# Decoder layer on one core: x turned by VectorE, three weights split in the mixing stage, the residual stored with its bias

## The chip, the cores and the metric

The kernel runs on one core of one Trainium2 chip. A core has TensorE (PE, matrix products), VectorE (DVE), ScalarE (ACT), GpSimd (POOL) and SyncE (SP), which here issues all the DMA transfers. Each engine works through its own queue in order, and semaphores are the only coupling between them. The metric is the device time of one execution in microseconds: 967.11 us before (median of 3 runs, 964.91 to 968.43). Lower is better.

## The reference

x is (8, 512, 512) in float32: 8 batches of 512 tokens. ctx is (8, 77, 512). The layer has three parts, each followed by a residual addition and a layer norm.

```python
# 1 mixing: 8 heads of 64
q, k, v = split(x @ w_qkv)
kv = cumsum(fft(k) * fft(v), over tokens)
x = layernorm(x + real(ifft(kv * conj(fft(q)))) @ w_out)
# 2 cross attention: 16 heads of 32 over 77 keys, masked softmax
q, k, v = x @ W_q + b_q, ctx @ W_k + b_k, ctx @ W_v + b_v
x = layernorm(x + softmax(mask(q k^T / sqrt(32))) v @ W_o + b_o)
# 3 feed forward with an int4-rounded weight and a low-rank term
w = clip(round(kernel / scale), -8, 7) * scale      # scale = max|kernel| / 7
x = layernorm(x + x @ w + bias + (x @ a) @ b)
```

## The kernel before, in words

Every float32 product is made as three products of a high part and a low part ("split": the high part is a copy to a format that TensorE reads in one pass, the low part is what is left): `split_matmuls` (L58) issues hi*hi, lo*hi and hi*lo for each of four 128-row chunks, so one product of a 128x512 tile is 12 matmuls. The program has three stages. Each ends in a barrier of all engines.

**prepare** (L69) works on weights. It folds the Fourier transform into w_qkv (PE turns 128x128 blocks of w_qkv, multiplies with the transform; the result is split into `w_spec`) and into w_out (`w_back`, `fold_back`), turns ctx and, in the last four entries of `SIDE` (L138), the x of batch 0; projects and stores the keys in 8 pieces (`project_keys`, `bias_keys`, `split_keys`, n = 0 to 7); rounds the FFN weight and adds the low-rank term (`merge`, L484). It also splits W_o, W_v and the finished FFN weight (ACT `split_o`, `split_v`, `split_ffn`; low parts on POOL and DVE) and stores the six parts to DRAM (`w_later`), in SP's queue between the keys' stores; the last two stores are L227 and L228. `partition_all_reduce` (L418) on POOL finds the largest |kernel|, and DVE waits for it before L498. The stage ends when SP has seen all its stores land.

**mix_tokens** (L570) takes one batch per step, i = 0 to 7; steps 2 to 5 are a loop of two. In a step PE makes twelve projections of 12 matmuls (2 pairs x {V, K, Q} x 2 halves) and four back projections (`project_back`) of the batch before. The first half of PE's order (L714) is V V K K Q, back 0, Q, back 1, V, back 2, V, back 3, and the second half K K Q Q. Between the first K, K, Q and back 0 stand four `turn` calls (L672), each four 128x128 transposes, which bring the x of the next batch into the bank `xT_ps`; ACT copies the high part (L780), DVE makes the low part (L899). DVE multiplies (`times_k`, `times_q`), runs the prefix sum (`scan`, L921 and L923), adds the residual x to a back projection (`add_residual`, L948), measures and normalises (L963); POOL adds the two halves of the values (L847), makes their low part (L853) and raises the variance to -1/2 (`root`, L838). `project_back(i, t)` waits for `r_added` of tile t-1, that is for DVE's `add_residual` of the tile before, since there is one bank `out_ps`. `add_residual(i, 0)` waits for the transfer into the single tile `x_res`.

The places that set SP's order are `load_x` (into two x tiles; the load of batch i+3 waits until batch i+1 is turned), `load_residual(i)` (waits until batch i-1 has used `x_res`) and `store` (four tiles of x1, waiting for DVE's normalised tiles).

**attend** (L1097) makes, per step, the scores of one batch and the output projections, FFN and norms of the batch before. Four PSUM banks are handed round in the order `BANK_ORDER` (L1030): `O0, P00, O1, P01, O2, T0, ...` are an output projection, a turned piece of the probabilities, and so on; the fifth use needs the first to be emptied. At the start of each step POOL adds b_o to the four tiles of the loaded residual (`bias_residual`, L1714) and only then scales the probabilities (`normalize_probs`, L1706), which PE turns in `turn_probs` (L1322). `add_o` (L1908) on DVE adds the biased residual. The first residual load (L1257) waits for all values to be stored, because both use one tile, and is queued behind 4 MB of weights.

## Time and profile before

| | us |
|---|---|
| median of 3 runs | 967.11 (964.91 to 968.43) |
| the profiled execution | 967.57 |
| its span, first to last instruction | 965.8 |

Busy shares of the span: PE 94%, PE's weight loads 78%, DVE 69%, ACT 39%, POOL 35%; the mean granted TensorE clock is 0.977 of full speed. A share is an average over three stages with different limits, so the rows below are given by stage. In a row of the timeline the first number is the start in us, the second the duration; brackets hold the idle time before it and what ended it. The stages begin at 0, 75.8 and about 464 us.

### The profile page before, as it was taken

What the parts mean: (1) busy time and instruction counts of PE and PEld (TensorE: products, weight loads), DVE (VectorE), ACT (ScalarE), POOL (GpSimd) and SP (SyncE); (2) the same over time, 40 slices, a digit from 0 to 9 for tenths busy, and PEclk for the clock granted to TensorE, in tenths of its full rate; (3) what the DMA queues carried; (4) which work ended last, traced back from release to release, by engine and by line L of the source; (5) the groups of instructions that cost most, each with busy time, mean ns of one, the idle gap of its engine ahead of it and who ended that gap; (6) DMA issues with size and microseconds to landing.
All of it is one profiled execution on the core that took longest, in us unless ns stands there. A gap on an engine that the chain in (4) does not pass through costs nothing.

```text
span 965.8 us, 14658 instructions
## 1 busy us (share of the span) xinstructions
PE 907.3 (94%) x4472; PEld 750.5 (78%) x4472; DVE 669.5 (69%) x1128; ACT 377.8 (39%) x1414; POOL 339.7 (35%) x312
## 2 busy tenths in 40 slices
PE   7848999999999999999797899999999999999997
PEld 7626888888888888888686788888888888888775
DVE  3863365656566666566575688979889798887957
ACT  6622211020111111001575466656567565666610
POOL 0230513131313232234231534444443444433733
PEclk9978999999999999999899899999999999999999
DMA  9894203030303010113738022131222203120021
GB/s 305 276 353 164 83 22 110 22 109 23 109 22 109 22 66 33 55 58 120 269 106 289 21 79 73 44 110 24 89 63 78 75 21 120 32 89 20 17 77 44
DMA packets 87388, 91.71 MB, mean 95 GB/s; under 512 B 42311, under 2 KB 48711, under 8 KB 87343
## 3 DMA queue, kind: packets, MB, share of 16 engines
q1 hardware_dynamic: 87343, 91.15, 28.9%
q8 instruction: 23, 0.38, 0.2%
q14 instruction: 22, 0.18, 0.1%
HBM read 60.50 MB, written 30.64 MB: 94 GB/s over the span
## 4 chain that ended last, share of the span: by engine, by line
PE 41%; issue 4%; POOL 2%; DVE 2%; ACT 1%; DMA 1%; SPq 0%; POOLq 0%; DVEq 0%
PE shared_ps L62 31%; PE score_ps L62 4%; PE shared_ps L1330 3%; POOL probs L1711 2%; PE shared_ps L1293 1%; PE shared_ps L1363 1%; ACT probs L1552 1%; DMA w_o_and_ffn<-weights_split 1%; DVE xT_and_qT L1819 0%; DVE x_and_res L1917 0%; POOL x_tok L1718 0%; POOL x_and_res L1726 0%; POOL rstd L1704 0%; DVE score_ps L1871 0%; SPq L1215 0%
## 5 line engine op out<-in xcount | busy, mean ns | idle before, releaser
L1552 ACT ACTIVATE probs<-score_ps,top_s 128x77 f32<-128x77 f32 x512 | 159.7, 357 | 31.2 <-DVE top_s L1876 31.0
L1552 ACT ACTIVATION_READ_ACCUMULATOR probs<-score_ps,top_s 128x1 f32 x512 | 122.2, 239 | 0.0
L1711 POOL TENSOR_TENSOR probs<-probs,per_total 128x616 f32<-128x616 f32 x64 | 82.7, 1308 | 68.8 <-DVE per_total L1883 68.7
L62 PE MATMUL shared_ps<-w_o_and_ffn,xT_and_qT 128*128 128x512 f32 x384 | 96.7, 400 | 4.1 <-DVE xT_and_qT L1819 3.4
L1704 POOL TENSOR_TENSOR rstd<-ve,half_power 128x1 f32<-128x1 f32 x64 | 42.2, 660 | 151.7 <-DVE ve L1906 147.2
L62 PE MATMUL shared_ps<-w_o_and_ffn,xT_hi 128*128 128x512 f32 x256 | 89.6, 413 | 2.3 <-DVE xT_lo L1827 1.8
L62 PEld LDWEIGHTS shared_ps<-w_o_and_ffn,xT_and_qT 128*128 128x128 f32 x384 | 70.1, 188 | 21.2 <-DVE xT_and_qT L1819 4.1
L838 POOL TENSOR_TENSOR mix_rstd<-mix_ve,half_power 128x1 f32<-128x1 f32 x32 | 22.1, 690 | 180.0 <-DVE mix_ve L956 180.0
L786 ACT ACTIVATE v_sb<-v_ps 128x512 f32<-128x512 f32 x32 | 19.1, 595 | 146.4 <-PE v_ps L62 146.4
L1559 ACT ACTIVATE pT_hi<-shared_ps 103x512 fp32r<-103x512 f32 (+1 forms) x96 | 54.5, 608 | 53.4 <-PE shared_ps L1330 52.9
L62 PE MATMUL out_ps<-w_back_hi,xT_and_qT 128*128 128x512 f32 x224 | 71.0, 398 | 0.0
L62 PE MATMUL score_ps<-xT_and_qT 128*128 128x308 f32 x384 | 66.0, 315 | 4.9 <-ACT probs L1552 2.9
L1855 DVE TENSOR_TENSOR pT_lo<-shared_ps,pT_hi 103x512 fp32r<-103x512 f32 (+1 forms) x96 | 64.7, 684 | 6.2 <-ACT pT_hi L1559 6.1
L793 ACT ACTIVATE xT_and_qT<-vals 128x512 fp32r<-128x512 f32 x32 | 19.4, 632 | 122.2 <-POOL vals L847 106.4
L1871 DVE COPY_PREDICATED score_ps<-hidden,masked 128x616 f32<-128x616 int32 x64 | 63.5, 992 | 5.1 <-PE score_ps L62 4.9
L62 PEld LDWEIGHTS score_ps<-xT_and_qT 128*128 128x128 f32 x384 | 59.4, 194 | 8.4 <-ACT probs L1552 3.3
L847 POOL TENSOR_TENSOR vals<-qs_prod 128x512 f32<-128x512 f32 x32 | 41.0, 1295 | 69.9 <-DVE qs_prod L937 69.9
L1330 PE MATMUL shared_ps<-ident,probs 128*103 128x128 f32 (+1 forms) x384 | 52.8, 275 | 11.1 <-POOL probs L1711 11.1
L62 PEld LDWEIGHTS shared_ps<-w_o_and_ffn,xT_hi 128*128 128x128 f32 x256 | 49.7, 194 | 14.9 <-issue 2.8
L1330 PEld LDWEIGHTS shared_ps<-ident,probs 128*103 128x103 f32 (+1 forms) x384 | 46.4, 156 | 18.0 <-POOL probs L1711 12.4
L1726 POOL TENSOR_TENSOR x_and_res<-x_and_res,bias_f 128x512 f32<-128x512 f32 x32 | 42.2, 1320 | 40.1 <-DVE x_and_res L1917 27.3
L1718 POOL TENSOR_TENSOR x_tok<-x_tok,bias_o 128x512 f32<-128x512 f32 x32 | 44.8, 1432 | 25.4 <-DMA x_tok<-x_between 25.4
(199 smaller groups left out, 2281.6 us busy)
## 6 DMA issues: line engine op xcount, KB each, us to landing
x_tok<-in_x SPq DMA_DIRECT2D x8, 1024.0 KB, 5.7
x_res<-in_x SPq DMA_DIRECT2D x8, 1024.0 KB, 7.8
x_between<-mix_x SPq DMA_DIRECT2D x32, 256.0 KB, 2.0
x<-x_between SPq DMA_DIRECT2D x8, 1024.0 KB, 5.6
x_tok<-x_between SPq DMA_DIRECT2D x8, 1024.0 KB, 5.7
out<-y_out SPq DMA_DIRECT2D x32, 256.0 KB, 2.0
w_o_and_ffn<-weights_split SPq DMA_DIRECT2D x6, 1024.0 KB, 8.6
weights_split<-wqkv_sb SPq DMA_DIRECT2D x4, 1024.0 KB, 5.5
```

The costliest lines, as they stand in the source:

```text
L62: last = nc.tensor.matmul(out, l, r, start=(n == 0), stop=(n == len(terms) - 1))
L838: nc.gpsimd.tensor_tensor(rstd[:, t % 2:t % 2 + 1], ve[:, t % 2:t % 2 + 1], half_power[:], ALU.pow).then_inc(rstd_ready, 1)
L847: nc.gpsimd.tensor_tensor(vals[:, h, :], qs[:, 2 * h, :], qs[:, 2 * h + 1, :], ALU.subtract if h else ALU.add).then_inc(vals_summed, 1)
L1330: last = nc.tensor.transpose(shared_ps[s.bank(use)][0:size, g * P:(g + 1) * P], probs[:, t % 2, g * GK + at:g * GK + at + size], ident[:])
L1552: nc.scalar.activation(probs[:, t % 2, j * KEYS:(j + 1) * KEYS], score_ps[:, g, k * KEYS:(k + 1) * KEYS], ACT.Exp, bias=top[:, t % 2, j:j ...
L1559: nc.scalar.activation(pT[0][0:size, c, :, t * P:(t + 1) * P], turned_bank(s, t, c), ACT.Copy).then_inc(turned_hi, 1)
L1704: nc.gpsimd.tensor_tensor(rstd[:, n:n + 1], ve[:, n:n + 1], half_power[:], ALU.pow).then_inc(rstd_ready, 1)
L1711: nc.gpsimd.tensor_tensor(p, p, per_total[:, t % 2, h * heads:(h + 1) * heads].unsqueeze(2) .to_broadcast([P, heads, KEYS]), ALU.mult).the ...
L1718: nc.gpsimd.tensor_tensor(res1[:, t, :], res1[:, t, :], bias_o[:], ALU.add).then_inc(res1_ready, 1)
L1726: nc.gpsimd.tensor_tensor(res2[:, t % 2, :], x2[:, t % 2, :], bias_f[:], ALU.add).then_inc(res2_ready, 1)
L1855: nc.vector.tensor_tensor(pT[1][0:size, c, :, tok], turned_bank(s, t, c), pT[0][0:size, c, :, tok].bitcast(F32), ALU.subtract).then_inc(fr ...
L1871: nc.vector.copy_predicated(s4, hidden[:, t, :].unsqueeze(1).unsqueeze(1).to_broadcast(shape), masked[:].unsqueeze(1).unsqueeze(1).to_broa ...
```

## The change

1. **x is turned by VectorE.** PE's transposes of x are gone, in prepare (16) and in mixing (four per call, four calls in each of steps 0 to 6). DVE's transpose turns 32x32 blocks only, so each x load becomes four transfers, one for each group of 32 partitions with runs of 128 columns (`load_blocks`), and w_qkv's rows are permuted to match where the Fourier transform is folded in. DVE writes to a new tile `x_turn` of two chunks. The split of x then reads `x_turn` instead of PSUM. There is one x tile instead of two, and the load of batch i+3 waits until batch i+2 is turned.
2. **W_v, W_o and the FFN weight are split in mixing.** prepare no longer loads W_v and W_o nor splits anything of the three; it stores the finished FFN weight once. In steps 0 and 1 of mixing each of the three is loaded into `x1_next`, split by ACT (high) and POOL (low), and stored in four high pieces and one low piece.
3. **x1 + b_o is stored by mixing.** POOL adds b_o after each normalised tile (`add_bias`), SP stores that tile as well (`res_dram`), attend loads the residual from there, and `bias_residual` is gone; `add_o` waits for the load itself.
4. w_qkv is loaded in six pieces of 512 KB instead of twelve of 256 KB.

```diff
+def load_blocks(sp, tile, rows, sem):
+    src = rows.rearrange("(u c) (a j) -> a c u j", c=BLOCK, a=P // BLOCK)
+    for a in range(P // BLOCK):
+        dst = tile[a * BLOCK:(a + 1) * BLOCK, :, :].rearrange("c t (k j) -> c (t k) j", j=P)
+        sp.dma_start(dst, src[a]).then_inc(sem, 16)
+def turn_block(nc, out, tile, b):
+    return nc.vector.transpose(out.rearrange("p (u c) -> p u c", c=BLOCK),
+                               tile[:].rearrange("p t (k b c) -> p (t k) b c", b=NC, c=BLOCK)[:, :, b, :])
...
@@ prepare, SP @@
-            sp.wait_ge(w_turned, 6)
+            sp.wait_ge(w_turned, NFOLD)
             sp.dma_start(ffn, by_chunk(ins["kernel"])).then_inc(kernel_loaded, 16)
-            sp.wait_ge(side_filled, N_CTX)
-            sp.dma_start(raw_o, by_chunk(ins["W_o"])).then_inc(wo_loaded, 16)
...
-            sp.dma_start(raw_v, by_chunk(ins["W_v"])).then_inc(wv_loaded, 16)
...
-            sp.wait_ge(ffn_lo, NC)
-            sp.dma_start(by_chunk(w_later[2, 0]), o_hi).then_inc(w_stored, 16)
-            sp.dma_start(by_chunk(w_later[2, 1]), ffn).then_inc(w_stored, 16)
+                if n == NKEY - 3:
+                    sp.wait_ge(merged_ready, NC)
+                    sp.dma_start(by_chunk(ffn_dram), ffn).then_inc(ffn_stored, 16)
...
@@ mixing, SP @@
-            load_x(1, 1, False)
-            sp.dma_start(x1_next[:], w_q_dram.rearrange("(c p) n -> p c n", p=P)).then_inc(wq_loaded, 16)
-            load_x(2, 0, False)
-            load_x(3, 1, True)
-            finish(0)
-            with sp.Fori(2, B - 3, 2) as i:
-                load_x(i + 2, 0, True)
-                finish(i - 1)
-                load_x(i + 3, 1, True)
+            load_x(1)
+            sp.dma_start(x1_next[:], by_chunk(w_q_dram)).then_inc(wq_loaded, 16)
+            load_residual(0)
+            load_x(2)
+            load_later(0)
+            store_later(0)
+            load_later(1)
+            store_later_hi(1, 0)
+            store_later_hi(1, 1)
+            load_x(3)
+            store_tile(0, 0)
+            store_tile(0, 1)
+            store_later_hi(1, 2)
+            store_later_hi(1, 3)
+            store_tile(0, 2)
+            store_tile(0, 3)
+            store_later_lo(1)
+            load_later(2)
+            store_later(2)
+            with sp.Fori(1, B - 3) as i:
+                load_x(i + 3)
                 finish(i)
...
+            def load_x(i):
+                wait_reuse(sp, xT_filled, (i - 1) * NC)
+                load_blocks(sp, x_tok, x[i], x_loaded)
...
@@ mixing, ACT @@
+            split_later(0, 2)
+            copy_v(1, 0, 0)
+            copy_v(1, 0, 1)
+            for c in range(NC):
+                split_x(2, 0, c)
+            split_later(1, 0)
+            copy_v(1, 1, 0)
+            copy_v(1, 1, 1)
+            split_later(1, 2)
+            for p in range(PAIRS):
+                for h in range(2):
+                    split_vals(1, p, h)
+            split_later(2, 0)
+            split_later(2, 2)
             steps(act, step)
...
@@ mixing, POOL: the end of step 0 and step 1 @@
+            split_later(0, 2)
+            split_later(1, 0)
+            for t in range(2):
+                root(0, t)
+                sum_vals(1, 0, t)
+            add_bias(0, 0)
+            add_bias(0, 1)
+            root(0, 2)
+            root(0, 3)
+            add_bias(0, 2)
+            add_bias(0, 3)
+            split_later(1, 2)
...
+            split_later(2, 0)
+            split_later(2, 2)
...
@@ mixing, DVE, step @@
-                turned(0)
+                if has_next:
+                    turn(i + 1, 1 - half, 0)
+                    turn(i + 1, 1 - half, 1)
                 times_k(i, 0, 0)
-                turned(1)
                 times_k(i, 0, 1)
-                turned(2)
+                if has_next:
+                    split_x(i + 1, 1 - half, 0)
+                    split_x(i + 1, 1 - half, 1)
+                    turn(i + 1, 1 - half, 2)
+                    turn(i + 1, 1 - half, 3)
                 scan(i, 0)
-                turned(3)
+                if has_next:
+                    split_x(i + 1, 1 - half, 2)
+                    split_x(i + 1, 1 - half, 3)
                 times_q(i, 0, 0)
                 if has_last:
                     add_residual(i - 1, 0)
...
@@ attend @@
-                sp.dma_start(res1[:], x1_dram[i].rearrange("(t p) d -> p t d", p=P)).then_inc(res1_loaded, 16)
+                sp.dma_start(res1[:], res_dram[i].rearrange("(t p) d -> p t d", p=P)).then_inc(res1_loaded, 16)
...
-                bias_residual(i - 1, 0)
-                bias_residual(i - 1, 1)
-                bias_residual(i - 1, 2)
-                bias_residual(i - 1, 3)
                 normalize_probs(i, 0, 0)
```

How the order of the instructions moves, at three places. First SP's queue in the loop of mixing, the loads of one turn. `x_tok` is the x tile, `x_res` the residual of the batch before. Before:

```order
L630 ISA
L631 ISA [waits xT_filled]
L631 DMA x_tok<-in_x 128x4x512
L636 ISA [waits r_added]
L636 DMA x_res<-in_x 128x4x512
L640 REGISTER_ALU
L641 DMA x_between<-mix_x 128x512 [waits x1_ready]
```

After:

```order
L75 ISA [waits xT_filled]
L75 DMA x_tok<-in_x 32x16x128
L75 ISA
L75 DMA x_tok<-in_x 32x16x128
L75 ISA
L75 DMA x_tok<-in_x 32x16x128
L75 ISA
L75 DMA x_tok<-in_x 32x16x128
L46 ISA
L581 ISA [waits r_added]
L581 DMA x_res<-in_x 128x4x512
L585 ISA
```

The residual stands behind the x load in both, but the count that this load waits for is one batch later, and there are four transfers in place of one.

Second, DVE in the first half of a step of mixing (step 6, which stands outside the loop), from the first work on the next batch's x to the first residual addition (`mix_r`). `kv_prod`, `state` and `qs_prod` are the products and the prefix sum. Before:

```order
L899 TENSOR_TENSOR xT_and_qT<-xT_ps,xT_and_qT 128x512 [waits x_hi]
L909 TENSOR_TENSOR kv_prod<-k_ps,v_sb 128x512 [waits scanned,v_copied,k_filled]
L910 TENSOR_TENSOR kv_prod<-k_ps,v_sb 128x512
L899 TENSOR_TENSOR xT_and_qT<-xT_ps,xT_and_qT 128x512 [waits x_hi]
L912 SCALAR_TENSOR_TENSOR kv_prod<-k_ps,sigma,v_sb 128x512 [waits scanned,v_copied,k_filled]
L914 TENSOR_TENSOR kv_prod<-k_ps,v_sb 128x512
L899 TENSOR_TENSOR xT_and_qT<-xT_ps,xT_and_qT 128x512 [waits x_hi]
L921 SCALAR_TENSOR_TENSOR state<-kv_prod 128x512 [waits qs_done,kv_done]
L923 SCALAR_TENSOR_TENSOR state<-kv_prod 128x512
L899 TENSOR_TENSOR xT_and_qT<-xT_ps,xT_and_qT 128x512 [waits x_hi]
L933 TENSOR_TENSOR qs_prod<-q_ps,state 128x512 [waits vals_summed,scanned,q_filled]
L934 TENSOR_TENSOR qs_prod<-q_ps,state 128x512
```

After:

```order
L80 STREAM_TRANSPOSE x_turn<-x_tok 128x512 [waits x_lo,x_hi,x_loaded0]
L80 STREAM_TRANSPOSE x_turn<-x_tok 128x512 [waits x_lo,x_hi]
L955 TENSOR_TENSOR kv_prod<-k_ps,v_sb 128x512 [waits scanned,v_copied,k_filled]
L956 TENSOR_TENSOR kv_prod<-k_ps,v_sb 128x512
L958 SCALAR_TENSOR_TENSOR kv_prod<-k_ps,sigma,v_sb 128x512 [waits scanned,v_copied,k_filled]
L960 TENSOR_TENSOR kv_prod<-k_ps,v_sb 128x512
L945 TENSOR_TENSOR xT_and_qT<-x_turn,xT_and_qT 128x512 [waits q_filled,xT_filled,x_hi] x2
L80 STREAM_TRANSPOSE x_turn<-x_tok 128x512 [waits x_lo,x_hi] x2
L967 SCALAR_TENSOR_TENSOR state<-kv_prod 128x512 [waits qs_done,kv_done]
L969 SCALAR_TENSOR_TENSOR state<-kv_prod 128x512
L945 TENSOR_TENSOR xT_and_qT<-x_turn,xT_and_qT 128x512 [waits q_filled,xT_filled,x_hi] x2
L979 TENSOR_TENSOR qs_prod<-q_ps,state 128x512 [waits vals_summed,scanned,q_filled]
```

Behind the second K product there stood two low parts of x before the residual addition; now four low parts and two transposes stand there.

Third, POOL at the beginning of attend, batch 0 and step 1 (`probs` are the probabilities, `x_tok` the residual, `rstd` a root). Before:

```order
L1756 MEMSET v_block_lo 103x1536
L1711 TENSOR_TENSOR probs<-probs,per_total 128x616 [waits exped,per_total_ready] x8
L1718 TENSOR_TENSOR x_tok<-x_tok,bias_o 128x512 [waits res1_loaded]
L1718 TENSOR_TENSOR x_tok<-x_tok,bias_o 128x512 x3
L1711 TENSOR_TENSOR probs<-probs,per_total 128x616 [waits exped,per_total_ready] x2
L1704 TENSOR_TENSOR rstd<-ve,half_power 128x1 [waits var_eps_b]
```

After:

```order
L1795 MEMSET v_block_lo 103x1536
L1760 TENSOR_TENSOR probs<-probs,per_total 128x616 [waits exped,per_total_ready] x10
L1753 TENSOR_TENSOR rstd<-ve,half_power 128x1 [waits var_eps_b]
L1769 TENSOR_TENSOR x_and_res<-x_and_res,bias_f 128x512 [waits x2_ready]
L1753 TENSOR_TENSOR rstd<-ve,half_power 128x1 [waits var_eps_b]
L1760 TENSOR_TENSOR probs<-probs,per_total 128x616 [waits exped,per_total_ready] x2
```

No wait for the residual stands ahead of the probabilities any more.

## Rows read from the trace of the kernel before

**Rows 1.** Windows by stage: us, busy us (instructions) of PE, PEld, DVE, ACT, POOL; clock; DMA share; GB/s.
```profile
0.00:75.80 75.80, 48.30 (x300) 40.91 (x301) 43.47 (x62) 34.12 (x65) 15.38 (x16) 0.91 0.92 306
75.80:458.00 382.20, 382.19 (x1696) 308.87 (x1697) 225.75 (x353) 59.32 (x102) 111.41 (x102) 0.99 0.20 69
...
600.00:900.00 300.00, 295.58 (x1575) 249.96 (x1575) 256.03 (x458) 182.14 (x803) 137.26 (x125) 1.00 0.22 62
```

**Rows 2.** Timeline of PE, step 1 of mixing and the start of step 2.
```profile
114.00 0.39 PE L62 MATMUL v_ps<-xT_and_qT,w_spec_hi 128*128 128x512 f32 x1
...
119.59 0.60 PE L680 MATMUL xT_ps<-ident,x_tok 128*128 128x128 f32 x4
...
160.51 0.40 PE L62 MATMUL v_ps<-xT_hi,w_spec_hi 128*128 128x512 f32 x1
```

**Rows 3.** Timeline of DVE, step 1 of mixing.
```profile
126.26 0.75 DVE L912 SCALAR_TENSOR_TENSOR kv_prod<-k_ps,sigma,v_sb 128x512 f32<-128x512 f32 x1 [1.35 <-PE k_ps L62]
...
128.12 1.22 DVE L921 TENSOR_TENSOR_SCAN state<-kv_prod 128x512 f32<-128x512 f32 x1
...
132.72 0.69 DVE L948 TENSOR_TENSOR mix_r<-out_ps,x_res 128x512 f32<-128x512 f32 x1 [0.28 <-PE out_ps L62]
...
152.38 1.50 DVE L963 TENSOR_SCALAR mix_x<-mix_r,mix_mv,mix_rstd 128x512 f32<-128x512 f32 x1 [0.44 <-POOL mix_rstd L838]
```

**Rows 4.** Timeline of SP's DMA issues in mixing.
```profile
154.62 0.42 SPq L631 DMA_DIRECT2D x_tok<-in_x  x1
155.32 0.40 SPq L636 DMA_DIRECT2D x_res<-in_x  x1
```

**Rows 5.** DMA issues, 154 to 165 us: KB each, us to landing.
```profile
x_res<-in_x SPq DMA_DIRECT2D x1, 1024.0 KB, 7.6
```

**Rows 6.** DMA issues of the whole span: KB each, us to landing.
```profile
weights_split<-wqkv_sb SPq DMA_DIRECT2D x4, 1024.0 KB, 5.5
keys_split<-xT_and_qT SPq DMA_DIRECT2D x16, 154.0 KB, 3.2
```

**Rows 7.** Timeline of PE, prepare and the start of mixing.
```profile
35.80 0.38 PE L62 MATMUL prod<-xT_and_qT,w_q_hi 128*128 128x308 f32 x1 [2.75 <-DVE w_back_lo L435]
...
75.81 0.77 PE L62 MATMUL v_ps<-xT_hi,w_spec_hi 128*128 128x512 f32 x1 [13.07 <-PEq L76]
```

**Rows 8.** The page's part 5: busy us, mean ns of one, idle before.
```profile
L786 ACT ACTIVATE v_sb<-v_ps 128x512 f32<-128x512 f32 x32 | 19.1, 595 | 146.4 <-PE v_ps L62 146.4
...
L847 POOL TENSOR_TENSOR vals<-qs_prod 128x512 f32<-128x512 f32 x32 | 41.0, 1295 | 69.9 <-DVE qs_prod L937 69.9
```

**Rows 9.** Timeline of SP, the last stores of prepare.
```profile
64.50 1.79 SPq L208 DMA_DIRECT2D keys_split<-xT_and_qT  x2
67.59 0.81 SPq L228 DMA_DIRECT2D weights_split<-wqkv_sb  x1
```

**Rows 10.** Timeline of DVE in prepare.
```profile
40.28 0.48 DVE L481 TENSOR_TENSOR xT_and_qT<-k_val,xT_and_qT 128x308 fp32r<-128x308 f32 x1 [0.15 <-DVE k_val L447]
...
40.68 0.15 DVE L498 TENSOR_SCALAR q_scale<-top_all 128x1 f32<-128x1 f32 x1
...
42.84 1.52 DVE L481 TENSOR_TENSOR xT_and_qT<-k_val,xT_and_qT 128x308 fp32r<-128x308 f32 x1 [0.15 <-DVE k_val L447]
...
58.91 1.28 DVE L490 TENSOR_TENSOR wqkv_sb<-wqkv_sb 128x512 fp32r<-128x512 f32 x2
```

**Rows 11.** Timeline of POOL in prepare.
```profile
34.00 0.38 POOL L418 PARTITION_ALL_REDUCE top_all<-top  x1 [32.34 <-DVE top L461]
```

**Rows 12.** Timeline of PE, step 1 of attend.
```profile
534.83 1.18 PE L1330 MATMUL shared_ps<-ident,probs 128*103 128x128 f32 x4 [9.20 <-POOL probs L1711]
...
539.73 0.39 PE L62 MATMUL shared_ps<-w_o_and_ffn,xT_lo 128*128 128x512 f32 x1
```

**Rows 13.** Timeline of SP, the residual's load in attend.
```profile
521.87 0.40 SPq L1188 DMA_DIRECT2D x_tok<-x_between  x1
```

**Rows 14.** Timeline of POOL, step 1 of attend.
```profile
527.51 4.92 POOL L1718 TENSOR_TENSOR x_tok<-x_tok,bias_o 128x512 f32<-128x512 f32 x4 [25.36 <-DMA x_tok<-x_between]
```

More of the change, by code:

```diff
@@ L131, in prepare @@
         NKEY = 2 * NC
-        GROUP = [(r, s) for r in range(NC) for s in range(3)]
+        GROUP = [(s, c) for s in range(3) for c in range(NC)]
         NFOLD = len(GROUP)
@@ L237, in turn @@
             def turn(n):
-                r, s = GROUP[n]
-                pe.wait_ge(qkv_loaded[r][s], 16)
+                s, c = GROUP[n]
+                pe.wait_ge(qkv_loaded[n // 2], 16)
                 wait_reuse(pe, wT_ready, n - 1)
-                for c in range(NC):
-                    at = s * D + c * P
-                    last = nc.tensor.transpose(turned[n % 2][:, c * P:(c + 1) * P], wqkv_sb[:, r, at:at + P], ident[:])
+                bank = turned[n % 2][:].rearrange("p (b a r) -> p a b r", b=NC, a=NC)
+                eye = ident[:].rearrange("p (b r) -> p b r", b=NC)
+                at = s * D + c * P
+                for a in range(NC):
+                    last = nc.tensor.transpose(bank[:, a], wqkv_sb[:, a, at:at + P], eye)
                 last.then_inc(w_turned, 1)
@@ L260, in turn_side @@
                                                    ident[0:tail_rows, 0:tail_rows])
-                else:
-                    for t in range(NT):
-                        last = nc.tensor.transpose(out[:, t * P:(t + 1) * P], x_first[:, t, c * P:(c + 1) * P], ident[:])
                 last.then_inc(side_filled, 1)
@@ L455, in _, with split_wk @@
                     split_side(m - FIRST_SIDE)
-            for c in range(NC):
+            def split_wk(c):
                 dve.wait_ge(wk_hi_ready, c + 1)
@@ L672, in _ @@
         def _(pe):
-            def turn(i, half, c):
-                if c == 0:
-                    pe.wait_ge(x_loaded[half], i_loads(i, half))
-                wait_reuse(pe, x_lo, nth(i - 1, NC, c - 1))
-                for t in range(NT):
-                    last = nc.tensor.transpose(xT_ps[:, t * P:(t + 1) * P], x_tok[half][:, t, c * P:(c + 1) * P], ident[:])
-                last.then_inc(xT_filled, 1)
-            def i_loads(i, half):
-                return (i - half) * 8 + 16
             def project(i, half, s, p, h):
@@ L779, in split_x, with split_later @@
                 act.wait_ge(xT_filled, nth(i - 1, NC, c))
[L780 removed]
+                wait_reuse(act, q_filled, (i - 1) * 4)
+                nc.scalar.activation(xT[half][0][:, c, :], x_turn[:, c % 2, :], ACT.Copy).then_inc(x_hi, 1)
+            def split_later(w, first):
+                act.wait_ge(later_loaded, 16 * (w + 1))
+                for c in (first, first + 1):
+                    wait_reuse(act, hi_stored[c % 2], 16 * (2 * w + c // 2))
+                    wait_reuse(act, later_lo, NC * w + c - 1)
+                    nc.scalar.activation(later[:, c % 2, :], x1_next[:, c, :], ACT.Copy).then_inc(later_hi, 1)
             def copy_v(i, p, h):
```

326 lines of the change are left out of this document (152 added, 174 removed).

## Prediction

> **What bounds the kernel now.** I read the windows by stage first. In mixing PE is busy 382.19 of 382.20 us and the DMA engines 20% of it; in the middle of attend PE is busy 295.58 of 300 [rows 1]. So there a microsecond counts only if PE's queue becomes shorter or PE waits. In prepare PE is busy 48.30 of 75.80 us and the DMA share is 0.92 [rows 1]: that stage ends with transfers, not with PE. I then read one step of mixing on PE, and DVE's work beside it, since PE's four back projections hang on DVE. Step 1 runs from 114.00 to 160.51, 46.51 us. Its first two products take 5.59 us, 2.795 each; sixteen are 44.72, which leaves 1.79 for the four turns of x [rows 2]. DVE starts the second K product at 126.26, which is as soon as K is there, and after one pair, two low parts and the prefix sum it has 0.28 us to spare before the back projection it adds the residual to [rows 3]. That is thin. SP comes third: the x load and the residual of batch 1 were issued at 154.62 and 155.32, in step 1, a step before the residual is used [rows 4]. The last view is where PE stands still: 13.07 us between prepare and mixing [rows 7] and 9.20 us in step 1 of attend [rows 12].
>
> **Prepare.** The stores of W_v, W_o and the FFN parts go, 6 MB, against one of 1 MB. SP's last issue was at 67.59, 0.81 us for two, and such a store lands in 5.5, so 73.5 to 73.9; mixing's first matmul is at 75.81, about 2.2 later [rows 6, 7, 9]. Now the last transfers are the two stores of the eighth key piece. They were issued at 64.50 in a pair of 1.79 us with nothing of the FFN ahead but its own queue [rows 9]. What moves DVE towards them: two of the four FFN low parts stood ahead of the eighth piece, 1.28 us [rows 10]; POOL no longer runs beside the keys' low parts, one of which took 1.52 us and the one before POOL began 0.48 (there are six such; I take 1.7 for all of them, bounds 0 and 6) [rows 10]. Against it: the largest |kernel| is now found behind the turning of x, about 3 us later. POOL's reduction began at 34.00 and DVE used it at 40.68 without waiting, so it took at most 6.7 [rows 10, 11]; the wait on DVE is 0 to 3.4, and I take 2, since PE fills part of it with the next key product. The kernel's own load waits for all twelve turned pieces instead of six, but SP's queue reached it only then anyhow. Sum: the last pair is issued about 62, lands 3.2 after its second issue [rows 6], and mixing starts near 67.5. **Gain 8.3 us**, bounds 6 and 12. The new gap of PE is still some 6 us, so I take the slow start of mixing (0.77 us for a matmul of 0.40) as unchanged [rows 7].
>
> **Mixing, the turns.** Seven steps lose 1.79 us of PE each [rows 2]. Without them a step is 44.72 us and PE, counted from its first matmul, has the second K at 11.2, back 0 at 16.8, and wants to begin back 1 at 19.6. That instruction waits for the first residual addition. DVE begins the second K product at 11.4. Before, the residual addition was ready 6.2 us later (132.72 less 0.28, less 126.26) [rows 3]. Now two more low parts and two transposes stand in between. A low part is an ordinary pass of 128x512, 0.69 [rows 3]. No DVE transpose is in the trace: it cannot cost less than nothing, and the slowest pass over one such tile is the prefix sum, 1.22 [rows 3]; I take the ordinary 0.69. So the addition begins at 11.4 + 6.2 + 2.8 = 20.4, ends at 21.1, and PE waits 1.5. The two early transposes lie in DVE's idle time ahead of the first K and cost nothing. **A step with only this: 1.79 gained, 1.5 lost** (bounds 0.1 and 2.6 lost). That holds for steps 1 and 6; step 0 has no back projection and keeps its 1.79, step 7 has neither.
>
> The Trainium skill, "VectorE: DVE Perf Modes", section "The three transpose paths", gives 311 ns for VectorE's transpose of a 128x128 tile in bf16, against 390 ns on TensorE. An estimate from that page is four times 311, 1.24 us for one of these passes. By the trace PE's own turn of the same data costs 1.79 us per step [rows 2]; by the page the move to DVE would be a loss wherever DVE is on the path. It is a rival below.
>
> **Mixing, the residual.** The single x tile makes the load of batch i+3 wait for the fourth transpose of batch i+2, which DVE makes in step i+1, and the residual of batch i stands behind it in SP's queue. Step i+1 is the step that uses this residual. So in steps 2 to 5 (the loop, i = 1 to 4; the residuals of batches 5 and 6 have no x load ahead of them and stay early) the residual is asked for at 11.4 + 1.2 (two K passes) + 4 x 0.69 = 15.4 us into the step and should be there at 20.4. Before, from the first issue to the landing of the residual it took 0.70 + 7.6 = 8.3 us [rows 4, 5]. Now three more issues stand ahead, at 0.70 each if nothing hides them [rows 4]: 8.3 to 10.4, and I take 9.5, since the data of the x load can move while SP issues. It lands at 24.9, the addition is done at 25.8 with its hops, and PE has waited since 19.6: **6.2 us**. Behind DVE's waiting addition stand the second Q product and the norms of the last batch, and behind PE's waiting back 1 the V projections; nobody else is late.
>
> Does the clock fall? After a stall of 9.20 us PE ran its turned piece and ten matmuls in 4.9 us, 534.83 to 539.73, where 0.45 + 10 x 0.233 = 2.8 is normal: 2.1 us lost [rows 2, 12]. After 2.75 us of waiting the first matmul, of 308 columns, took 0.38, against 0.77 for the one of 512 behind the 13.07 [rows 7]: no loss is seen there. 6.2 lies between, a little nearer to 9.2: I take 2.1, bounds 0 and 2.1. A step with a late residual is then 6.2 + 2.1 - 1.79 = 6.5 us longer.
>
> Step 2 has one more. The FFN weight's split stands in ACT's queue at the end of step 1, ahead of the V copies of step 2, and its load waits on a chain: the fourth tile of batch 0 normalised at 39.9 after the step's start (152.38 + 1.50 - 114.00) [rows 2, 3], now about 39.6; three POOL passes of 1.3 [rows 8] to 43.5; the low half of W_o stored, 5.5, and the FFN weight loaded, about the same [rows 6], to 54.5. Step 2 starts at 46.2, so ACT begins the split 8.3 us into it, needs four copies of 0.6 with two POOL passes between [rows 8], and then the two V copies: 13.3, where DVE wants them at 8.6. DVE catches up part of it and is 3.3 late at the second K product, and with it the residual's request.
>
> **Mixing in sum:** -1.8 (step 0) - 0.3 (1) + 9.8 (2) + 3 x 6.5 (3 to 5) - 0.3 (6) = **+26.9 us**. POOL's 32 additions of b_o, SP's 32 more stores and the six weight stores lie beside PE; POOL is busy 111 of 382 us [rows 1].
>
> **Attend.** POOL waited 25.36 us for the residual, which SP issued at 521.87, and only then came the bias and the probabilities that PE waited 9.20 us for [rows 12 to 14]. Now POOL does not wait. DVE does, at the first output projection, until the residual lands at 527.5 [rows 14]. PE ends that projection at 534.83 - 9.20 = 525.6, goes on with a turned piece, the next projection and a piece (0.45 + 2.8 + 0.45) to 529.3, and only then needs the bank that DVE empties by 528.3. So nothing takes the place of the stall, and 9.20 and the 2.1 of the slow clock behind it go: **gain 11.3 us**, bounds 8 and 12. In the other steps POOL's freed passes release nobody, since PE is busy 98.5% [rows 1].
>
> **Sum.** 967.57 for the profiled execution, less 8.3, less 11.3, plus 26.9: 974.9. It was 0.5 above the median of the runs, so 974.5, rounded to 975.
>
> **Rivals.** (A) *The residual is never late* and the change is a clear gain. Place: SP's queue in the loop. It decides at 5.0 us from request to landing (15.4 to 20.4). Mixing then gains 1.8 + 6 x 0.3 = 3.6 and the whole is 944. Against it: 7.6 us for the residual behind one x load [rows 5]. Only a reading error of mine about the wait would bring it; 0.12. (B) *Late, but cheap:* landing after 8.3 and no loss of clock. The steps lose 5.0 instead of 8.3: mixing +13.7, time 962; 0.18. (C) *The x load in four takes longer than in one.* From rows alone: the residual itself took 7.6 where the x load ahead took the same bytes; if the x load's moving time of some 2.4 us doubles, each of four stalls grows by 2.4, time 984; 0.12. The Trainium skill, "SBUF — State Buffer", section "Door 1: The DMA port swizzle", says that a transfer to 32 partitions reaches 8 of the 16 ports and that two transfers are not fused, which would bring just this; no run here shows it yet. (D) *The transpose takes as long as the prefix sum*, 1.22: two on the path in six steps, 6.4 more, 981; 0.08. It is the case of the 1.24 above. My forecast has 0.50.
>
> **How the numbers follow.** The likeliest case by itself is 968 to 982. Cases of both signs hold chance, so the range is 953 to 987: it takes in B, C and D and leaves out A and the far tail. What this kernel's measurement can tell from no change is about 0.5%, that is 962.3 to 971.9. Slower: 0.42 of the forecast's 0.50, C and D, 0.62. Faster: A, 0.10 of B and 0.02 of the forecast, 0.24. Within: what is left of B and of the forecast, 0.14.
>
> **What would show it.** In the new profile: mixing's first matmul near 67.5; on DVE a wait of `mix_r` for the DMA of `x_res` of 4 to 5 us in each of four steps, and a wait of PE's `out_ps` for DVE of about 6 there, with slow matmuls behind; steps 3 to 5 of 53 us, steps 1 and 6 of 46.2; ACT's V copies of step 2 at 12 us into it; no wait of POOL for the residual in attend and no stall of PE at the first turned piece. I am wrong if the residual lands before DVE asks for it, if the clock stays up behind the stalls, or if prepare ends as late as before.

## The result, and the profile after

| | before | after |
|---|---|---|
| median | 966.15 us (20 runs, 963.56 to 969.26) | 969.74 us (20 runs, 966.21 to 974.21) |
| ratio | | 1.0039, 95% interval 1.0024 to 1.0053 |
| profiled execution, and its span | 967.57, 965.8 | 969.73, 967.9 |

The change makes the kernel slower, by 0.39%. The forecast was 975, or 0.8%. It had the direction, but twice the size. The median lies inside the 0.5% that the prediction took for what can be told from no change, a case to which it gave a chance of 0.14. Twenty runs of each tell the two kernels apart all the same.

The windows by stage come first. They answer to [rows 1].

```profile
0.00:71.00 71.00, 48.30 (x284) 38.98 (x285) 37.22 (x58) 28.31 (x53) 6.80 (x12) 0.90 0.78 224
71.00:479.50 408.50, 379.65 (x1600) 303.38 (x1600) 256.01 (x385) 67.02 (x116) 171.38 (x147) 0.97 0.35 110
600.00:900.00 300.00, 296.71 (x1587) 252.00 (x1586) 250.62 (x462) 183.47 (x815) 106.80 (x105) 1.00 0.22 63
```

Over the whole of mixing, 75.80 to 463.90, PE was busy 386.12 of 388.10 us in the kernel before; the 2.0 us are the pause ahead of attend. Now it is idle for 28.9 of 408.5 us, the same 2.0 among them, and its mean clock is lower. In attend PE is a little busier. Who PE waits for is in the waits of PE over the whole span (us in total, times, longest):

```profile
PE out_ps L62 <- DVE mix_r L994: 26.9, 6, 8.2
PE turned L272 <- DMA a_sb<-in_a: 6.8, 1, 6.8
PE turned L236 <- DMA wqkv_sb<-in_w_qkv: 6.7, 2, 5.4
PE score_ps L62 <- ACT probs L1601: 5.2, 1, 5.2
...
PE v_ps L62 <- PEq L91: 3.2, 1, 3.2
```

The first line is new: six waits of the second back projection for the first residual addition. The last answers to the 13.07 of [rows 7]. Three of the six on PE's timeline, with the first matmul of steps 2 and 3 between them, answer to [rows 2]:

```profile
125.12 0.50 PE L62 MATMUL out_ps<-w_back_hi,xT_and_qT 128*128 128x512 f32 x1 [0.66 <-DVE mix_r L994]
...
150.41 0.40 PE L62 MATMUL v_ps<-xT_hi,w_spec_hi 128*128 128x512 f32 x1
...
178.34 0.79 PE L62 MATMUL out_ps<-w_back_hi,xT_and_qT 128*128 128x512 f32 x1 [8.16 <-DVE mix_r L994]
...
205.49 0.40 PE L62 MATMUL v_ps<-xT_and_qT,w_spec_hi 128*128 128x512 f32 x1
...
230.84 0.79 PE L62 MATMUL out_ps<-w_back_hi,xT_and_qT 128*128 128x512 f32 x1 [5.58 <-DVE mix_r L994]
```

Step 2 takes 205.49 - 150.41 = 55.08 us. Step 1 began at 104.70 and takes 45.71. A matmul of 0.79 behind a wait runs at half the clock of the 0.40 ones. Whom DVE waits for, in mixing and in step 3:

```profile
DVE mix_r L994 <- DMA x_res<-in_x: 20.3, 4, 5.3
DVE x_turn L80 <- DMA x_tok<-in_x: 8.4, 1, 8.4
DVE kv_prod L955 <- ACT v_sb L765: 8.2, 1, 8.2
...
224.58 0.68 DVE L980 TENSOR_TENSOR qs_prod<-q_ps,state 128x512 f32<-128x512 f32 x1
230.09 0.69 DVE L994 TENSOR_TENSOR mix_r<-out_ps,x_res 128x512 f32<-128x512 f32 x1 [4.83 <-DMA x_res<-in_x]
```

Four waits for the late residual, longest 5.3, and one for ACT's late V copies. SP's queue in the same step shows the order that the change made; it answers to [rows 4]:

```profile
220.84 1.95 SPq L75 DMA_DIRECT2D x_tok<-in_x  x4
223.08 0.40 SPq L581 DMA_DIRECT2D x_res<-in_x  x1
```

The first issue is at 15.35 us into the step and the addition starts 9.25 us behind it. The clock behind the four long waits is in the windows of the back projection that follows each. Twelve matmuls take 2.80 at full clock:

```profile
178.34:183.10 4.76, 4.76 (x13) 3.76 (x13) 2.31 (x5) 0.00 (x0) 1.83 (x2) 0.57 0.01 3
230.84:235.01 4.17, 4.17 (x13) 3.32 (x13) 2.31 (x5) 0.00 (x0) 1.84 (x2) 0.66 0.00 0
283.22:288.41 5.19, 5.19 (x13) 4.09 (x13) 2.32 (x5) 0.00 (x0) 1.83 (x2) 0.51 0.00 0
336.37:340.67 4.30, 4.30 (x13) 3.42 (x14) 2.32 (x5) 0.00 (x0) 1.84 (x2) 0.64 0.00 0
```

In prepare the x load in four held SP for 8.24 us where one transfer had held it for 3.07, and the first keys left at 47.33 where it had been 40.83. These are SP's issues in the kernel before:

```profile
12.10 3.07 SPq L183 DMA_DIRECT2D x_tok<-in_x  x1
...
40.83 0.82 SPq L208 DMA_DIRECT2D keys_split<-xT_and_qT  x2
```

In the changed kernel (SP's issues, then DVE; the last two rows stand against [rows 9, 10]) DVE waited 2.95 us for POOL's reduction, and the stage ended with the key stores. The row at 66.18 is the pair of the eighth piece:

```profile
14.21 8.24 SPq L75 DMA_DIRECT2D x_tok<-in_x  x4
22.49 1.44 SPq L192 DMA_DIRECT2D wout_sb<-in_w_out  x1
...
47.33 0.82 SPq L209 DMA_DIRECT2D keys_split<-xT_and_qT  x2
...
66.18 1.90 SPq L209 DMA_DIRECT2D keys_split<-xT_and_qT  x2
...
50.25 0.15 DVE L443 TENSOR_SCALAR q_scale<-top_all 128x1 f32<-128x1 f32 x1 [2.95 <-POOL top_all L371]
```

In attend, DVE's addition of the first residual waited 1.60 us. PE did not wait where it had stood for the 9.20 of [rows 12]; at 550.62 it waited 1.61 us, once, for DVE's low part of another tile, where the kernel before waits 0.6:

```profile
536.81 0.41 SPq L1237 DMA_DIRECT2D x_tok<-residual_between  x1
...
542.71 0.69 DVE L1926 TENSOR_TENSOR y<-shared_ps,x_tok 128x512 f32<-128x512 f32 x1 [1.60 <-DMA x_tok<-residual_between]
```

Step by step, from the first matmuls on PE's timeline of both traces:

| term | forecast | measured |
|---|---|---|
| mixing's first matmul | -8.3 | -4.8 (75.81 to 71.03) |
| the slow clock behind it | 0 | -2.7 (step 0: 38.19 to 33.67, less the turns) |
| turns of step 0 | -1.8 | -1.8 |
| steps 1 and 6, together | -0.6 | -1.6 (45.71 each) |
| step 2 | +9.8 | +8.6 |
| steps 3, 4, 5 | +19.5 | +18.0 (5.4, 6.9, 5.7) |
| attend, the first residual | -11.3 | -11.3 |
| attend, the other steps | 0 | -2.2 |
| sum | +7.3 | +2.2 |

### The profile page after: what moved, and what is told of

It is laid out like the page before. It is cut to its first block, busy times and chain, and to the rows that moved or that the text cites. A ratio compares the mean times of both kernels' runs of the same rounds, so it can differ in the third digit from the quotient of the medians.

```text
span 967.9 us, 14663 instructions
## 1 busy us (share of the span) xinstructions
PE 895.2 (92%) x4344; PEld 737.5 (76%) x4344; DVE 683.1 (71%) x1152; ACT 377.2 (39%) x1414; POOL 346.8 (36%) x320
## 4 chain that ended last, share of the span: by engine, by line
PE 42%; DMA 3%; DVE 2%; POOL 1%; issue 1%; ACT 1%; SPq 0%; POOLq 0%; DVEq 0%
PE shared_ps L62 32%; PE score_ps L62 4%; PE shared_ps L1379 4%; PE shared_ps L1342 1%; PE shared_ps L1412 1%; POOL probs L1760 1%; DMA values_split<-x_tok 1%; DMA w_o_and_ffn<-weights_split 1%; DMA x_tok<-residual_between 1%; DVE x_and_res L1948 0%; DVE xT_and_qT L1850 0%; ACT probs L1601 0%; POOL x_and_res L1769 0%; DVE y L1926 0%; POOL rstd L1753 0%
## 5 line engine op out<-in xcount | busy, mean ns | idle before, releaser
L62 PE MATMUL out_ps<-w_back_hi,xT_and_qT 128*128 128x512 f32 x224 | 76.3, 424 | 26.9 <-DVE mix_r L994 26.9
L62 PEld LDWEIGHTS out_ps<-w_back_hi,xT_and_qT 128*128 128x128 f32 x224 | 45.1, 204 | 40.2 <-DVE mix_r L994 29.5
L772 ACT ACTIVATE xT_and_qT<-vals 128x512 fp32r<-128x512 f32 x32 | 19.5, 631 | 124.0 <-POOL vals L839 109.2
L994 DVE TENSOR_TENSOR mix_r<-out_ps,x_res 128x512 f32<-128x512 f32 x29 | 20.0, 691 | 66.6 <-PE out_ps L62 46.4
L1902 DVE COPY_PREDICATED score_ps<-hidden,masked 128x616 f32<-128x616 int32 x64 | 56.4, 881 | 4.8 <-PE score_ps L62 4.6
```

Of the source, the lines that this page charges most:

```text
L62: last = nc.tensor.matmul(out, l, r, start=(n == 0), stop=(n == len(terms) - 1))
L994: nc.vector.tensor_tensor(r_sb[:, k, :], bank[:], x_res[:, t, :], ALU.add).then_inc(r_added, 1)
L1902: nc.vector.copy_predicated(s4, hidden[:, t, :].unsqueeze(1).unsqueeze(1).to_broadcast(shape), masked[:].unsqueeze(1).unsqueeze(1).to_broa ...
```

## The experiments

Ten kernels ran. Their times stand beside runs of the kernel before on the same chip (966.3 to 967.2 us). The diffs show the main place of each edit; "..." marks what is left out.

**1. The residual asked for early.** In the changed kernel:

```diff
             def finish(i):
-                load_residual(i)
                 store(i)
+                load_residual(i + 1)
...
             store_tile(0, 3)
+            load_residual(1)
             store_later_lo(1)
             load_later(2)
...
-            load_residual(B - 1)
```

> The changed kernel, with the residual of batch i+1 asked for at the end of step i+1's stores of batch i instead of behind the x load in the next step. Nothing else moves. Theory L (the late residual costs the steps): PE's waits of 8.2, 5.6, 6.0 and 5.8 us and the slow matmuls behind them (2.0, 1.4, 2.4, 1.5) go, so steps 3 to 5 fall from 51.9, 53.4 and 52.3 us to the 45.7 of steps 1 and 6, and step 2 from 55.1 to about 48.5, since its V copies on ACT are still late and DVE reaches the addition some 3 us late. Together 27 us less: about 943 us. Rival D (DVE's two more low parts and two transposes on the path are what PE waits for, and the residual only seems last): PE still waits 3 to 6 us in each of the four steps, and the time stays above 958.

Measured: 945.97 us, ratio 0.9785 (0.976 to 0.9809). Steps 3 to 6 take 45.71 us each, step 2 takes 51.05.

```profile
175.70 0.50 PE L62 MATMUL out_ps<-w_back_hi,xT_and_qT 128*128 128x512 f32 x1 [4.45 <-DVE mix_r L993]
...
222.96 0.50 PE L62 MATMUL out_ps<-w_back_hi,xT_and_qT 128*128 128x512 f32 x1 [0.66 <-DVE mix_r L993]
```

Theory L holds: what the change lost in mixing hung on the place of one load in SP's queue, some 24 us. Step 2 kept more than the 48.5 expected: DVE's first K product waited 9.65 us for the V copies and began 14.0 us into the step (12.5 in the changed kernel). The residual load now stands ahead of the last store of W_o and of the FFN weight's load in SP's queue, and that load was issued 4.0 us into the step in place of 1.5.

**2. The FFN weight's split behind the V copies of step 2**, on top of 1:

```diff
+            copy_v(2, 0, 0)
+            copy_v(2, 0, 1)
+            split_x(3, 1, 0)
+            split_x(3, 1, 1)
             split_later(2, 0)
             split_later(2, 2)
-            steps(act, step)
+            split_x(3, 1, 2)
+            split_x(3, 1, 3)
+            copy_v(2, 1, 0)
+            copy_v(2, 1, 1)
...
```

> The residual early as in the first run, and in addition ACT's split of the FFN weight stands behind the first two V copies and two high parts of x of step 2 instead of ahead of them. Theory A (the split ahead of the V copies costs step 2): the second K product on DVE no longer starts 2.4 us late and step 2 comes down to 45.7 to 46.2, so 2 to 3 us less than the first run: about 940.5. Rival P (the split costs the same wherever it stands, since POOL's four low parts of 1.27 us are now ahead of the first root of the step): no gain, 943 again, with a wait of DVE for POOL's root in step 2.

Measured: 944.14 us, 0.9768 (0.975 to 0.9786). The interval overlaps that of run 1, so the time alone doesn't show the gain. The traces do: step 2 falls from 51.05 to 48.92, with 2.33 us of wait left. Theory A holds in part: 45.7 to 46.2 was expected. The second K product no longer waited for the V copies, but two low parts behind it took 2.96 us where two take 1.28 elsewhere (the last section).

**3. The late load alone, in the kernel before:**

```diff
-                    sp.wait_ge(xT_filled, nth(i - 3, NC, NC - 1))
+                    sp.wait_ge(xT_filled, nth(i - 2, NC, NC - 1))
...
             load_x(2, 0, False)
+            load_residual(0)
             load_x(3, 1, True)
-            finish(0)
+            store(0)
```

> The kernel before, with only SP's wait for the x load made one batch later, as the changed kernel has it (the residual of batch 0 is asked for first, so steps 2 to 5 are the ones touched). Theory L: the fourth turn ends 15.6 us into the step, the residual lands 8.3 us later at 23.9 to 24.2, is added by 24.9, and PE, which wants the second back projection at 21.3, waits 3.5 to 4 us in each of four steps: 14 to 16 us more if the clock stays up, 980 to 982; with 1.4 to 2.4 us of slow matmuls behind each, up to 990. Rival N: the residual was never the limit, and the time stays at 966.

Measured: 987.53 us, 1.0219 (1.0202 to 1.0237), in the upper part of the expectation. The trace is of the slowest of the five runs, 990.77. The first of the four waits and the clock of the twelve matmuls behind it:

```profile
186.70 0.80 PE L62 MATMUL out_ps<-w_back_hi,xT_and_qT 128*128 128x512 f32 x1 [3.27 <-DVE mix_r L949]
...
186.70:191.98 5.28, 5.28 (x12) 4.13 (x13) 2.31 (x5) 0.00 (x0) 1.82 (x2) 0.50 0.00 0
```

The four waits are 3.27, 3.97, 3.33 and 4.02, 14.6 us. The four steps are longer by 6.2, 5.8, 5.1 and 6.8, 23.8 us. So a wait of 3.3 to 4.0 us was paid with 1.7 to 2.9 us more, of matmuls at 1.2 GHz. The mechanism needs neither the transposes nor the four-part load.

**4. Only x1 + b_o stored by mixing, in the kernel before** (part 3 of the change, with its stores, `add_bias` and `add_o`). No diff is shown; it is that part alone.

> The kernel before, with only the third part of the change: POOL adds b_o behind each normalised tile of mixing, the sum is stored, and attend loads the residual with its bias. Theory S (the whole gain of attend, 13.6 us between the two traces, is this part): mixing stays at 46.5 us a step, and attend is 13.6 us shorter: 11.3 at the first residual and 0.43 in each of five later steps (58.30 against 58.72), where POOL's four passes of bias are gone: about 952.5. Rival H (the 0.43 per step has another cause, such as where DVE's work falls): 11.3 only, 955. Rival M: 32 more POOL passes and 32 more stores in mixing make its steps longer, by what is missing from 13.6.

Measured: 953.75 us, 0.9874 (0.9856 to 0.9892). Mixing's steps stay at 46.51, so the 32 passes and stores cost nothing there. The later steps of attend, at the same matmul, take 58.27:

```profile
591.12 0.49 PE L62 MATMUL shared_ps<-w_o_and_ffn,xT_and_qT 128*128 128x512 f32 x1 [0.57 <-DVE xT_and_qT L1817]
...
649.39 0.49 PE L62 MATMUL shared_ps<-w_o_and_ffn,xT_and_qT 128*128 128x512 f32 x1 [0.57 <-DVE xT_and_qT L1817]
```

Between the same matmuls the kernel before took 663.10 - 604.36 = 58.74 and the changed one 58.30. Theory S holds: part 3 alone takes 12.6 us off the kernel before, by the medians, where attend's gain between the two traces is 13.5, and it can be had without the rest.

**5 to 7. How the x load is cut.** In the changed kernel `load_blocks` became four transfers of another form, each of 256 KB: `tile[:, a:a+1, :]` (all partitions, runs of 2 KB), `tile[32a:32a+32, :, :]` (32 partitions, 2 KB) and `tile[:, :, 128a:128a+128]` (all partitions, 512 bytes). They leave out the order of the tokens that the transpose needs, so they don't compute the layer; the work is the same.

> The changed kernel with another cut of each x load into four transfers: one of 128 tokens each, over all 128 partitions in runs of 2 KB, in place of 32 partitions in runs of 512 bytes. The tokens land in another order, so what is computed from x is not the layer's; the work is the same. In the changed kernel the load moved at 200 to 230 GB/s, the whole residual behind it at 380 to 400. Theory C (the cut costs the rate): the x load moves in some 2.6 us in place of 4.7, the residual lands 7.4 to 8.3 us after the first issue in place of 9.5, PE waits 1.2 to 2 us less in each of steps 2 to 5, and in prepare the weights behind the x load arrive 2 to 3 us sooner: 7 to 10 us less than the changed kernel, 960 to 963. Rival I (four issues cost, not the form of the bytes): no difference, 969.7.

> As the run before, with the four transfers over 32 partitions each as in the changed kernel, but in runs of 2 KB (tokens in another order again). If the 32 partitions set the rate, the load moves at 200 to 230 GB/s as in the changed kernel; if the runs of 512 bytes do, at 380 or more.

> As the two before, with each transfer over all 128 partitions in runs of 512 bytes (a quarter of the columns; the order of the columns is kept, the order of tokens isn't). If the 32 partitions set the rate, the load moves at 380 or more; if the short runs do, at 200 to 230.

The window from 14 to 24 us, in prepare, where the load meets a full queue, in the changed kernel and the three, in this order (the last number is GB/s):

```profile
14.00:24.00 10.00, 8.70 (x80) 8.51 (x79) 5.18 (x9) 7.32 (x16) 0.00 (x0) 1.00 1.11 275
```

```profile
14.00:24.00 10.00, 10.00 (x92) 10.00 (x91) 5.67 (x10) 8.70 (x18) 0.00 (x0) 1.00 1.07 382
```

```profile
14.00:24.00 10.00, 10.00 (x94) 10.00 (x92) 5.66 (x10) 8.68 (x17) 0.00 (x0) 1.00 1.09 283
```

```profile
14.00:24.00 10.00, 9.65 (x88) 9.46 (x87) 5.63 (x9) 8.27 (x17) 0.00 (x0) 1.00 1.06 334
```

| | first keys stored | last two pairs of key stores begin | x load lands, in a loop step | PE's wait, steps 2 to 5 |
|---|---|---|---|---|
| 32 partitions, 512 bytes | 47.33 | 64.41 | 4.1 | 8.2, 5.6, 6.0, 5.8 |
| all, 2 KB | 39.71 | 56.35 | 3.2 | 8.1, 6.4, 5.2, 6.4 |
| 32, 2 KB | 46.21 | 62.85 | 4.5 | 7.8, 6.0, 5.6, 5.7 |
| all, 512 bytes | 42.40 | 59.04 | 3.2 | 8.6, 6.2, 7.1, 7.0 |

So the 32 partitions set the rate, and the short runs take a smaller share. The changed kernel and runs 1 and 2 have the same prepare, and show how far one execution may differ from another: 275, 276 and 292 GB/s in this window, and the first keys stored at 47.33, 47.68 and 43.99. The whole rows stored them at 39.71, so the cut cost 4 to 8 us, and theory C is right in prepare; the first keys of runs 6 and 7, one execution each, can't be ranked within such a spread. How long SP is held by the four issues follows the runs and not the partitions (2.83, 2.86 and 6.54 us in runs 5 to 7, 8.24 in the changed kernel). It isn't what made the keys late: run 6 held SP for 2.86 and stored its first keys at 46.21. Theory C is wrong in mixing: each piece lands 0.9 us sooner and PE waits as long as before, since the residual behind it takes longer (7.8 us from its issue in place of 7.0, in step 3). Why the residual is slower then stays open. The whole rows were also timed: 966.93 us (12 runs, 960.39 to 972.81), 1.0001 (0.998 to 1.0022), against the 1.0039 of the changed kernel. That is 3 to 4 us of the 7 to 10 expected: its part in mixing is missing, and its runs spread widely. The profiled execution was one of its fastest, 962.06. Runs 6 and 7 ran once each, in 968.74 and 967.62 us, from which no time can be compared.

**8. The first x load behind the weights**, on top of 2. In prepare SP loads it behind the FFN kernel, DVE turns it behind the first two key pieces, and ACT and POOL split it later too:

```diff
-            load_blocks(sp, x_first, ins["x"][0], hand.x_loaded)
...
             sp.dma_start(ffn, by_chunk(ins["kernel"])).then_inc(kernel_loaded, 16)
+            load_blocks(sp, x_first, ins["x"][0], hand.x_loaded)
...
             split_keys(0)
+            dve.wait_ge(hand.x_loaded, 16 * P // BLOCK)
+            dve.wait_ge(w_turned, NFOLD)
+            for c in range(NC):
+                turn_block(nc, x_turn[:, c, :], x_first, c).then_inc(x_turned, 1)
             dve.wait_ge(top_spread, 1)
```

> The second run's kernel with the first x load, in prepare, moved in SP's queue behind w_out, the low-rank factors and the FFN kernel, and the turning and splitting of batch 0 moved behind the first two key pieces, where DVE waited 2.95 us for POOL's reduction. Theory Q (the x load of 8.2 us in SP's queue is why prepare ended at 71.0 and not at 67.5): w_out lands 6 to 8 us sooner, PE no longer waits 6.8 us for the low-rank factors, the first keys are stored near 41 to 42 us in place of 47.3, and step 1 of mixing starts at 98 to 101 us in place of 103 to 106: 3 to 5 us less than the second run, about 940. Rival W (DVE's and ACT's own work sets the keys, and the four turns in the middle of it delay them as much as they save): 944.

Measured: 937.44 us, 0.9693 (0.9671 to 0.9716). The first keys leave at 37.61 and step 1 of mixing starts at 99.16. Theory Q holds. Runs 9 and 10, with the same prepare, stored the first keys at 37.61 and 38.62, against 44.0 to 47.7 in the three executions with the old order, so 5.4 us at least are the edit's at that place; at the start of step 1 it is 98.50 to 99.47 against 103.12 to 105.77. The gain on run 2 is 6.7 us by the medians, above the 3 to 5 expected.

**9. Two low parts behind the residual addition**, on top of 8:

```diff
-                if has_next:
-                    split_x(i + 1, 1 - half, 2)
-                    split_x(i + 1, 1 - half, 3)
                 times_q(i, 0, 0)
                 if has_last:
                     add_residual(i - 1, 0)
+                if has_next:
+                    split_x(i + 1, 1 - half, 2)
+                    split_x(i + 1, 1 - half, 3)
```

> The kernel of the run with x behind the weights, and in mixing DVE makes the low parts 2 and 3 of the next x behind the first residual addition instead of ahead of it. Theory O (what is left of DVE's order is a wait of 0.66 us and 0.25 of slow matmuls in each step): steps 1 and 3 to 6 fall from 45.71 to the 44.80 of sixteen products, and the wait in step 2, 2.8 us, by 1.3: 6 us less, about 931.5. Rival Z (the two low parts then delay the second Q product and the additions 1 to 3, and the wait only moves to the third back projection): 937.

Measured: 932.56 us, 0.9651 (0.9635 to 0.9667). Steps 3 to 6 take 44.80, which is sixteen products and nothing else; step 2 takes 45.83. Theory O holds there. Step 1 stayed at 45.59, where 44.80 was expected: the two low parts took 3.42 us beside POOL's low parts of W_o, and PE waited 0.54 us at the third back projection, which is what rival Z had named.

**10. The FFN weight's split in the middle of step 2**, on top of 9, on ACT (below), POOL and SP:

```diff
...
             copy_v(2, 1, 0)
+            split_later(2, 0)
             copy_v(2, 1, 1)
+            split_later(2, 2)
```

> The run before, and the split of the FFN weight moved to the middle of step 2: ACT makes the high parts behind its third and fourth V copies, POOL the low parts behind the roots of the batch before, SP stores them between that batch's tiles. In the run with x behind the weights, two low parts of x on DVE took 3.45 us in place of 1.28 while POOL worked on the FFN weight. Theory X (that overlap and ACT's place in the queue are all that makes step 2 longer): step 2 falls to 44.8 like the others, from 49.38 in that run: 2 to 4 us less than the run before, about 928.5. Rival Y (POOL's four passes are as dear wherever they stand, since DVE works there too): no gain.

Measured: **930.64 us, 0.9628 (0.9613 to 0.9642)**, the lowest median of all. Step 2 is now like the others, by the windows of steps 1 to 3:

```profile
99.47:144.86 45.39, 45.07 (x193) 35.93 (x192) 33.85 (x48) 10.10 (x18) 26.69 (x22) 1.00 0.54 173
144.86:189.67 44.81, 44.81 (x193) 36.02 (x192) 32.67 (x49) 9.04 (x16) 25.47 (x21) 1.00 0.47 146
189.67:234.46 44.79, 44.79 (x194) 36.01 (x192) 32.60 (x50) 6.87 (x12) 20.23 (x17) 1.00 0.43 136
```

The traces give 1.0 us for step 2 (45.83 to 44.81), as theory X says of the step; of the 49.38 in run 8 that it started from, run 9 had already taken 3.6, so the 2 to 4 us expected were no longer there. Against run 9 the times leave the gain unclear, since the intervals overlap; both are faster than the kernel before and the changed one.

## Why the prediction was right or wrong

**Right in mechanism.** The late residual was the main term, and runs 1 and 3 show it from both sides. The request was forecast at 15.4 us into a step and came at 15.35; the residual was to land at 9.5 us, and the addition came 9.25 behind the first issue; the wait of 6.2 was 5.6 to 6.0 in steps 3 to 5. The V copies of step 2 were forecast at 12 us and began at 11.4. The stall in attend was worth 11.3, as forecast: from the first scores to the same point of step 2, 128.74 us became 117.41. That figure is in part luck, since it holds the longer wait at 550.62 and the freed passes of that step, which the forecast had not.

Rivals A, B and D are refuted: the residual was late in four steps, the clock fell behind each of the waits, and the 28 transposes took 0.69 us each:

```profile
L80 DVE STREAM_TRANSPOSE x_turn<-x_tok 128x512 f32<-128x512 f32 x28 | 18.2, 689 | 8.4 <-DMA x_tok<-in_x 8.4
```

The 1.24 us estimated from the Trainium skill, "VectorE: DVE Perf Modes", section "The three transpose paths", was nearly twice too long for this form; here the measurement decides.

**Wrong in size, by 5.1 us,** through four terms, of which one is off the other way:

- *Mixing, steps 1 to 6: 28.7 forecast, 25.0 measured.* The step that failed first is the price of DVE's path: 0.69 each for the "two more low parts and two transposes", on top of 6.2 us. A pass of 0.69 is followed by the next after 0.60 to 0.65 (the two low parts at 117.36 take 1.28 together), and a prefix sum of 1.19 after 1.10. From the second K product to the addition it was 8.28 us, not 9.0, so PE waited 0.66 in steps 1 and 6, not 1.5. That is 1.0 of the 3.7 us. Step 2 holds 1.2: DVE was 2.3 us late there, not 3.3. Steps 3 to 5 hold 1.5: step 3's addition ended 25.3 us into the step, not at 25.8, and the slow clock cost 1.5 to 2.6, not 2.1 throughout.
- *"In the other steps POOL's freed passes release nobody, since PE is busy 98.5%": 0 forecast, -2.2 measured.* The 1.5% left of 300 us is 4.4 us, and 0.44 us of each step of 58.74 went with those passes, as run 4 shows.
- *Prepare: -8.3 forecast, -4.8 measured.* The step that failed is "the last pair is issued about 62"; it was issued at 66.18. The terms given there don't make 62: 64.50 less 1.28 and 1.7, plus the wait of 2, is 63.5. The wait was 2.95. And the sum took what drops out at the end of the stage and left the x load's new form out at its start; rival C was weighed for mixing alone. The Trainium skill, "SBUF — State Buffer", section "Door 1: The DMA port swizzle", says that 32 partitions reach 8 of 16 ports; runs 5 and 6 agree in direction, 382 against 283 GB/s. In mixing, where I had put it, it didn't shorten PE's waits.
- *"I take the slow start of mixing ... as unchanged": 0 forecast, -2.7 measured.* The first matmul of mixing took 0.47 in place of 0.77, and step 0 was 2.7 us shorter than the turns explain. PE's gap fell from 13.07 to 3.2 us, but that isn't shown to be the cause. Behind gaps of 3.0 to 3.2 us the first matmul took 0.47 in the changed kernel and in runs 5 and 7, and 0.77 in run 6, where step 0 was 1.3 us longer (35.01 against 33.67):

```profile
69.23 0.77 PE L62 MATMUL v_ps<-xT_hi,w_spec_hi 128*128 128x512 f32 x1 [2.97 <-PEq L90]
```

The last two terms belong to one pair of executions. Step 1 began at 114.00, 115.42 and 112.35 in the traces of the kernel before and of runs 3 and 4, which have its prepare, and at 104.70, 105.77 and 103.12 in those of the changed kernel and of runs 1 and 2. The means are 9.4 us apart; the forecast for prepare and step 0 together was 10.1. So up to there it was nearly right, by two errors that cancel in part, and what fails beyond the spread of the executions is mixing's steps and the later steps of attend.

Each error by itself is small; in a sum of -8, -11 and +27 they are as large as what is left.

## What to carry to other kernels

When a buffer is taken away, look at what stands in the DMA queue behind the load that now waits, not only at that load: here one residual load behind it cost 24 us, and asking for it at the end of the step before gave that back. Price a wait of TensorE with the clock behind it: in the middle of mixing, waits of 2.3 us and more cost 1.5 to 2.9 us more than themselves. On a critical path, count the distance from start to start of an engine's passes, not their durations, and read a share of 98.5% as microseconds before writing that nobody waits. Before a term of a few microseconds in a stage that moves data is called wrong or right, look at the same code in other executions: here the start of step 1 moved by 2.7 us between three of them.
